# TensorE's side jobs dealt anew over the eight slots of an attention and FP4 feed-forward kernel

## The reference

```python
xn = _layernorm(x)
q  = rope((xn @ Wqa @ Wqb).reshape(b, s, 16, 8))
kv = (xn @ Wkva @ Wkvb).reshape(b, s, 4, 8, 2); k, v = rope(kv[..., 0]), kv[..., 1]
w  = softmax(causal(einsum('bqhd,bkhd->bhqk', q, repeat(k, 4)) * 8 ** -0.5))
attn = einsum('bhqk,bkhd->bqhd', w, repeat(v, 4)).reshape(b, s, 128) @ Wout + bout
h   = silu(fp4_linear(xn, w_gate)) * fp4_linear(xn, w_up)      # 352 hidden features
out = x + attn + fp4_linear(h, w_down)
```

## Time and profile before

| | |
|---|---|
| median of 3 runs | 909.72 us (909.21 to 912.68) |
| profiled execution | 912.46 us, of which the span is 910.7 us |
| mean granted TensorE clock | 0.979 |
| PE busy | 760.9 us, 84% |
| DVE busy | 633.5 us, 70% |
| POOL busy | 595.6 us, 65% |
| ACT busy | 554.4 us, 61% |

### The profile page before, as it was taken

How to read it: one execution, slowest core, us unless ns; L and a number is a source line. 1 busy time by engine, 2 the same in 40 slices (tenths; PEclk the granted TensorE clock), 3 DMA queues, 4 the chain that set the end, 5 groups by cost and what they waited for, 6 DMA issues and landing times.

```text
span 910.7 us, 21907 instructions
## 1 busy us (share of the span) xinstructions
PE 760.9 (84%) x6641; PEld 479.6 (53%) x6733; DVE 633.5 (70%) x1380; ACT 554.4 (61%) x1169; POOL 595.6 (65%) x706
## 2 busy tenths in 40 slices
PE   2366879989897989989897988989898898999785
PEld 1233545656564555646555565645655565656344
DVE  3679877687776867767786778768776877777300
ACT  1122766675756766665675667566666667575761
POOL 3425778776775667857676687666676887664731
PEclk9998999999999999989999999999999999999997
DMA  4312122323223132321222232221223232220000
GB/s 113 92 53 83 46 79 62 89 64 84 56 62 77 29 89 63 89 52 60 72 65 66 54 89 58 75 70 53 60 53 90 63 89 53 70 70 13 15 24 12
DMA packets 66257, 58.28 MB, mean 64 GB/s; under 512 B 17298, under 2 KB 56178, under 8 KB 66170
## 3 DMA queue, kind: packets, MB, share of 16 engines
q1 hardware_dynamic: 66170, 57.04, 23.8%
HBM read 31.81 MB, written 18.61 MB: 55 GB/s over the span
## 4 chain that ended last, share of the span: by engine, by line
PE 40%; ACT 18%; issue 13%; DVE 11%; POOL 9%; another core or an unknown queue 4%; SPq 2%; DMA 1%; DVEq 1%; ACTq 0%; POOLq 0%
PE pv_ps L1036 8%; ACT P L840 6%; PE exp_ps L1017 6%; DVE neg_max L646 5%; PE misc_ps L1103 5%; PE max_ps L1002 5%; POOL P L495 5%; PE misc_ps L1054 4%; PE misc_ps L1064 3%; ACT h_mag L948 2%; PE max_ps L1003 2%; PE misc_ps L1072 2%; PE misc_ps L1101 2%; ACT hqT L886 1%
## 5 line engine op out<-in xcount | busy, mean ns | idle before, releaser
L646 DVE TENSOR_REDUCE neg_max<-max_ps 128x1 f32<-128x512 f32 (+3 forms) x768 | 430.6, 596 | 183.8 <-PE max_ps L1003 182.4
L840 ACT ACTIVATE P<-exp_ps 128x512 f32<-128x512 f32 x512 | 291.7, 599 | 200.2 <-PE exp_ps L1017 103.6
L1017 PE MATMUL exp_ps<-Q,K 128*128 128x128 bf16 (+3 forms) x932 | 211.6, 295 | 25.4 <-ACT P L840 18.3
L1002 PE MATMUL max_ps<-K,Q 128*128 128x384 bf16 (+2 forms) x768 | 200.3, 280 | 35.3 <-DVE neg_max L646 15.6
L1003 PE MATMUL max_ps<-Kd,Q 128*128 128x128 bf16 x1024 | 191.4, 222 | 0.7 <-DVE neg_max L646 0.5
L1036 PE MATMUL pv_ps<-P,V 128*32 128x512 f32 (+3 forms) x2048 | 167.0, 442 | 18.6 <-POOL P L495 12.9
L495 POOL TENSOR_SCALAR_AFFINE_SELECT P<-P 128x512 f32<-128x512 f32 x256 | 153.9, 638 | 19.0 <-ACT P L843 19.0
L1002 PEld LDWEIGHTS max_ps<-K,Q 128*128 128x128 bf16 x768 | 76.9, 100 | 111.8 <-issue 52.2
L1003 PEld LDWEIGHTS max_ps<-Kd,Q 128*128 128x128 bf16 x1024 | 101.0, 99 | 37.2 <-issue 19.3
L1017 PEld LDWEIGHTS exp_ps<-Q,K 128*128 128x128 bf16 x1024 | 79.3, 98 | 73.7 <-ACT P L840 48.4
L1036 PEld LDWEIGHTS pv_ps<-P,V 128*32 128x32 f32 x2048 | 59.5, 110 | 78.9 <-issue 45.5
(11 more groups left out here) (113 smaller groups left out, 1013.5 us busy)
## 6 DMA issues: line engine op xcount, KB each, us to landing
Q<-q_scr SPq DMA_DIRECT2D x64, 224.0 KB
q_scr<-q_split SPq DMA_DIRECT2D x16, 384.0 KB, 2.6
Kd<-K SPq DMA_DIRECT2D x64, 96.0 KB
x_in<-x SPq DMA_DIRECT2D x16, 256.0 KB, 2.9
q_scr<-q_split SPq DMA_DIRECT2D x16, 256.0 KB, 2.9
x_res<-x SPq DMA_DIRECT2D x16, 256.0 KB, 5.4
out<-y SPq DMA_DIRECT2D x16, 256.0 KB, 4.5
K<-k_scr SPq DMA_DIRECT2D x64, 48.0 KB
```

The costliest lines, as they stand in the source:

```text
L646: nc.vector.tensor_reduce(neg_max[:, pr // 4, i, heads[0]:heads[0] + len(heads), pr % 4], max_ps[r % 3][:, 0:len(heads) * n].rearrange("p ...
L840: nc.scalar.activation(P[g % 2][:, hh + r % 2, col:col + 512], ps[:, :], ACT.Exp, scale=SCALE).then_inc(exp_done, 1)
L1002: nc.tensor.matmul(ps[:, col:col + d], Qt, Kt[:, half, g, 0:d], start=True, stop=True)
L1017: last = nc.tensor.matmul(exp_ps[n % 2][:, col:col + width], K[par][:, half, pr // 2, kb * 128:(kb + 1) * 128], Q[par][:, pr, kb * 128:S], ...
```

## The change

- `MISC`: mrow1 from bank 1 to bank 0. Slot 2 has q at point 0, qrot at point 1 and ot1 at point 2; kv goes to slot 3, point 1; onT to slot 4, point 1. The output job is cut into out0 (slot 5, point 0) and out1 (slot 6, point 0), of two token blocks each. xqT and ot0 go to bank 1, mrow0 to bank 0, and hqT0, hqT1 and hqT2 stand at the three points of slot 7.
- Weighted sums: key blocks 0 and 3 in even slots, 1 and 2 in odd ones.
- ACT's h_mag pieces at (6, 2), (6, 4), (7, 0) and (7, 2). The rest of ACT's `extra` is as it was.
- DVE: its reads stand at new places, y is made in halves, and ot0 is read from bank 1.
- SP: the store is two DMAs, one ahead of and one behind `place_max(T, 1, 0)`; POOL's x_bias waits for out1 of the step before.

```diff
 MISC = [
     [[("gate0", 0, 1), ("up0", 1, 1)], [], []],
-    [[("gate1", 0, 1), ("up1", 1, 1)], [("xnT", 1, 2)], [("mrow1", 1, 0)]],
-    [[("q", 0, 2), ("qrot", 1, 2)], [("ot1", 0, -1), ("kv", 1, 2)], []],
-    [[("gate2", 0, 1), ("up2", 1, 1)], [("onT", 1, -1)], []],
-    [[("gate3", 0, 1), ("up3", 1, 1)], [], []],
-    [[("out", 0, -1)], [("xqT", 0, 2)], []],
-    [[("hqT0", 1, 0)], [("ot0", 0, 0), ("hqT1", 1, 0)], [("mrow0", 1, 1)]],
-    [[("hqT2", 1, 0)], [], []],
+    [[("gate1", 0, 1), ("up1", 1, 1)], [("xnT", 1, 2)], [("mrow1", 0, 0)]],
+    [[("q", 0, 2)], [("qrot", 1, 2)], [("ot1", 0, -1)]],
+    [[("gate2", 0, 1), ("up2", 1, 1)], [("kv", 1, 2)], []],
+    [[("gate3", 0, 1), ("up3", 1, 1)], [("onT", 1, -1)], []],
+    [[("out0", 0, -1)], [("xqT", 1, 2)], []],
+    [[("out1", 0, -1)], [("ot0", 1, 0)], [("mrow0", 0, 1)]],
+    [[("hqT0", 1, 0)], [("hqT1", 0, 0)], [("hqT2", 1, 0)]],
 ]
-H_POWERS = [(6, 2), (6, 3), (6, 4), (7, 0)]
+H_POWERS = [(6, 2), (6, 4), (7, 0), (7, 2)]
+PV_BLOCKS = ((0, 3), (1, 2))
...
                 if T.has(-1):
-                    T.misc_wait(sp, misc_read, "out")
-                    sp.dma_start(out[T.batch(-1)].rearrange("(c p) e -> p c e", p=128), y[:, :, :]).then_inc(stored, 16)
+                    store(T, 0)
                 if T.has(1):
                     place_max(T, 1, 0)
+                if T.has(-1):
+                    store(T, 1)
...
-                reduces(2, 2)
+                reduces(2, 2, 3)
                 if T.has(2):
                     T.misc_wait(dve, misc_filled, "qrot")
...
-                reduces(2, 3)
+                reduces(2, 4, 5)
+
+                reduces(3, 0)
                 normalize(T, -1, 1)
-                reduces(2, 4)
+                reduces(3, 1)
+                hidden_max(T, 1)
+                reduces(3, 2)
+                gated(T, 2)
+                reduces(3, 3, 4)
                 if T.has(2):
...
                     nc.vector.tensor_copy(v_stage[:, :, :], ps[:, 256:384].rearrange("p (c n) -> p c n", c=NT)).then_inc(misc_read[1], 1)
-                reduces(2, 5)
-
-                reduces(3, 0, 1)
-                hidden_max(T, 1)
-                reduces(3, 2)
-                gated(T, 2)
-                reduces(3, 3, 4)
+                reduces(3, 5)
+
+                reduces(4, 0, 1)
...
-                    T.wait(dve, stored, 16, -1, 0)
-                    nc.vector.tensor_tensor(y[:, :, :], misc_ps[0][:, :].rearrange("p (c e) -> p c e", c=NT),
-                                            x_bias[:, :, :], ALU.add).then_inc(misc_read[0], 1)
+                    T.wait(dve, stored, 32, -1, 0)
+                    output(T, 0)
                 reduces(5, 3)
...
-                reduces(6, 0, 1, 2, 3)
+                reduces(6, 0, 1, 2)
+                if T.has(-1):
+                    output(T, 1)
+                reduces(6, 3, 4)
                 normalize(T, 0, 0)
-                reduces(6, 4, 5)
-
-                reduces(7, 0, 1, 2)
+                reduces(6, 5)
+
+                reduces(7, 0, 1, 2, 3)
                 if T.has(1):
                     T.wait(dve, h_powers, NT, 1, NT)
                     magnitudes(lambda s, n: T.wait(dve, s, 2, 1, n), h_mag[:, :], h_mags)
-                reduces(7, 3, 4, 5)
+                reduces(7, 4, 5)
...
-                for kb in ((2, 3) if second else (0, 1)):
+                for kb in PV_BLOCKS[second]:
...
-                elif job == "out":
+                elif job in ("out0", "out1"):
                     T.misc_wait(pe, misc_read, "onT")
-                    for c in range(NT):
-                        nc.tensor.matmul(ps[:, tok[c]], onT[:, tok[c]], wout_sb[:, :], start=True, stop=False)
+                    for n in range(2):
+                        c = 2 * int(job[-1]) + n
+                        nc.tensor.matmul(ps[:, tok[n]], onT[:, tok[c]], wout_sb[:, :], start=True, stop=False)
```

More of the change, by code:

```diff
@@ L414, in copy_k, with store @@
                     sp.dma_start(Kd[r:r + MROW, half, gs, :], K[i][r:r + MROW, half, gs, :]).then_inc(qk_loaded[hf], 16)
+            def store(T, n):
+                T.misc_wait(sp, misc_read, f"out{n}")
+                rows = out[T.batch(-1)].rearrange("(c p) e -> p c e", p=128)
+                sp.dma_start(rows[:, 2 * n:2 * n + 2, :], y[:, 2 * n:2 * n + 2, :]).then_inc(stored, 16)
             def place_max(T, off, hf):
@@ L551, in iteration @@
                     T.wait(pool, x_res_loaded, 16, -1, 16)
-                    T.prev().misc_wait(pool, misc_read, "out")
+                    T.prev().misc_wait(pool, misc_read, "out1")
                     nc.gpsimd.tensor_tensor(x_bias[:, :, :], x_res[:, :, :],
@@ L682, in normalize, with output @@
                 nc.vector.tensor_tensor(o_norm[:, :, g, :, :],
-                                        misc_ps[0][:, :].rearrange("p (c n d) -> p c n d", c=NT, d=16)[:, :, :, 0:D],
+                                        misc_ps[1 - g][:, :].rearrange("p (c n d) -> p c n d", c=NT, d=16)[:, :, :, 0:D],
                                         o_inv[:, :, :].rearrange("p (c j) s -> p c (j s)", c=NT).unsqueeze(3).to_broadcast([128, NT, 8, D]),
-                                        ALU.mult).then_inc(misc_read[0], 1)
+                                        ALU.mult).then_inc(misc_read[1 - g], 1)
+            def output(T, n):
+                T.misc_wait(dve, misc_filled, f"out{n}")
+                c = slice(2 * n, 2 * n + 2)
+                nc.vector.tensor_tensor(y[:, c, :], misc_ps[0][:, 0:2 * E].rearrange("p (c e) -> p c e", c=2),
+                                        x_bias[:, c, :], ALU.add).then_inc(misc_read[0], 1)
             def iteration(T):
@@ L757, in iteration @@
                     magnitudes(lambda s, n: T.wait(dve, s, 2, 2, n), x_mag[:, :], x_mags)
-                reduces(3, 5)
-                reduces(4, 0, 1, 2)
+                reduces(4, 2)
                 gated(T, 3)
-                reduces(4, 3)
+                reduces(4, 3, 4)
                 hidden_max(T, 2)
-                reduces(4, 4, 5)
+                reduces(4, 5)
                 reduces(5, 0, 1)
@@ L1037, in weighted_sums @@
                                                 P[g % 2][:, j, P_COL[kb]:P_COL[kb] + width],
-                                                start=(kb == 0 and g % 2 == 0), stop=(kb == NT - 1 and g % 2 == 1))
+                                                start=(kb == 0 and g % 2 == 0), stop=(kb == PV_BLOCKS[1][1] and g % 2 == 1))
                 if second:
@@ L1050, in misc_job @@
                     f = int(job[-1])
-                    if bank == 1:
-                        T.prev().misc_wait(pe, misc_read, "xqT")
+                    T.prev().misc_wait(pe, misc_read, "xqT")
                     last = nc.tensor.matmul(ps[:, 0:F], xqT[T.par(1)][:, tok[f]], wguT[:, int(job[0] == "u"), :], start=True, stop=True)
@@ L1059, in misc_job @@
                 elif job in ("q", "qrot"):
-                    if bank == 0:
-                        T.misc_wait(pe, misc_read, "xnT")
+                    T.misc_wait(pe, misc_read, "xnT")
                     c0 = E * int(job == "qrot")
@@ L1096, in misc_job @@
                         last = nc.tensor.transpose(ps[:, tok[c]], o_norm[:, c, :, :, :].rearrange("p g n d -> p (g n d)"), ident[:, :])
-                elif job == "out":
+                elif job in ("out0", "out1"):
                     T.misc_wait(pe, misc_read, "onT")
-                    for c in range(NT):
-                        nc.tensor.matmul(ps[:, tok[c]], onT[:, tok[c]], wout_sb[:, :], start=True, stop=False)
+                    for n in range(2):
+                        c = 2 * int(job[-1]) + n
+                        nc.tensor.matmul(ps[:, tok[n]], onT[:, tok[c]], wout_sb[:, :], start=True, stop=False)
                         for k, (_, cn) in enumerate(FC):
-                            last = nc.tensor.matmul(ps[:, tok[c]], hqT[0:cn, k, tok[c]], wdT[0:cn, k, :], start=False, stop=(k == 2))
+                            last = nc.tensor.matmul(ps[:, tok[n]], hqT[0:cn, k, tok[c]], wdT[0:cn, k, :], start=False, stop=(k == 2))
                 last.then_inc(misc_filled[bank], 1)
```

5 lines of the change are left out of this document (2 added, 3 removed).

## The result

The changed kernel takes 968.12 us (median of 5 runs, 962.91 to 969.92) beside 910.7 of the kernel before (5 runs): a ratio of 1.0595, 95% interval 1.0565 to 1.0625. The profiled execution is the fastest of the five, 962.91 us, with a span of 961.2 against 910.7 before. The mean granted clock of TensorE fell from 0.979 to 0.940.

A forecast was written before the change was run, and what follows sets the result against it. An iteration was taken as the sum over its eight slots of whichever engine is last in each. Slot changes gave +2.85 us an iteration, +40 over 14 iterations, -2 for two more: +38, 948 us; range 912 to 983.

The forecast's parts named there:

- The mechanism, slot 3: Late kv delays k_rope and ScalarE's cast; PE stands idle before the fifth exp tile; slot 9.9 against 4.93, +5.0 us.
- the waits in slot 5: Slot 5: DVE waits 1.6 us at h_scale for POOL's product of the old h; xqT no longer waits for y.
- the signs named: ScalarE idle some 4 us, k_rope waiting over 5, PE gap over 2, slot 3 near 10, slots 2, 4, 5 under 6.
- The sum at full clock: Slot changes of one iteration, +0.1 +0.6 -2.1 +5.0 -0.4 -2.3 +1.2 +0.75, add to +2.85 us.
- rival B: Clock falls in every slot 3: 14 x 1.2 = 17 us more, 965 us, up to 983; chance 0.25.
- between those rows but nearer the first: Slot 3's new gap, about 2.7 us, set between a 2.87 gap with low clock and a 1.76 gap with full clock.
- PE waits for POOL in slot 4 anyway: Argument against the fallen clock's cost: slot 4 has PE waiting for POOL in any case; no size given.
- A: Stall in slot 3 with the clock kept: 948 us, bounds 912 to 967; chance 0.55.
- Rival C: k_rope ready before ACT needs it, so no slot 3 stall: -1.65 us an iteration, 885 us; chance 0.14.
- Levelled sums at nothing: Pairing key blocks 0+3 and 1+2: even slots lose 0.4 us, odd ones gain 0.4, so no net gain.
- The sum over two slots stays: Weighted sums of an even and an odd slot together take unchanged time, about 1.2 us each after the change.

The follow-up runs named there:

- the run with the cast later: Changed kernel with ScalarE's cast of k_rope behind its fifth exp tile and GpSimd's k_rope and k_rest behind other work: 906.56 us, ratio 0.9904.
- the version with the mask first: The run with the cast later, plus normalize(ot1) earlier, h scales behind slot 5's reductions, GpSimd's causal mask before its h_inv product, h_mag pieces later: 869.66 us, ratio 0.9515.

## Why the prediction was right, and where it was wrong

**The mechanism, slot 3: right.** ScalarE's stall (3.86 us, "some 4" foreseen), k_rope's wait (7.17), PE's gap before the fifth exp tile (2.72, foreseen 2.7) and the slot (10.11 at full clock, foreseen 9.9) are as worked out; so are the waits in slot 5, and TensorE no longer waits for y there. Of the signs named, one failed by a little: slot 2 is 6.1 to 6.2 us, not under 6. Moving kv alone into the kernel before gives ratio 1.0506, and back out of the changed one 1.0004.

**The sum at full clock: right.** The slots of T=13, foreseen and measured: 6.1 and 6.03; 7.2 and 6.61 (this iteration had 6.07 before, so it is +0.5 of the +0.6 foreseen); 5.85 and 6.21; 9.9 and 10.11; 5.7 and 5.76; 5.7 and 5.74; 7.75 and 7.42; 5.1 and 5.23. The step grew by 2.61 us, foreseen 2.85; single slots miss by up to 0.6 us, and these misses nearly cancel.

**The clock: rival B happened, not the 948 us with the clock kept.** The failing step is the weighing of the new gap as "between those rows but nearer the first", from which I still gave the kept clock 0.55 against 0.25. Behind 12 of 14 gaps of 2.54 to 2.72 us it fell. All four turns of the loop in the kernel before spoke for that, and I showed only one of them; "PE waits for POOL in slot 4 anyway" had no row behind it. But length was not the whole of the rule either: four gaps of 2.44 to 2.87 us of the changed kernel kept the clock. The measured 968 lies above the upper bound of A, 967, and is in the range by B alone. B's price, 1.2 us an iteration and 965 us in all, was near it, in part by luck: slots 3 and 4 lost 2.2 together in T=11 (11.68 + 6.39 against 10.11 + 5.76), less in others, 20 in all. The low clock lasts into slot 4, where 0.81 is its mean; I had priced it in the sums alone, 17 us. Against that stands what I had not foreseen: at the loop's turns the changed kernel kept the clock that the kernel before lost, so slots 0 and 1 behind them take 11.5 us together in place of 12.2 to 13.3, 4 us in all. The Trainium skill, page "TensorE: Matmul & The Clock Gate", section "HAM oscillation — how this bites in real kernels", has a loop in which each pass starts cold, and the waits of that loop are longer than this gap. The low clock in each pass is what came here, but for two passes of fourteen.

**Rival C, 885 us without the stall: wrong in its price.** With TensorE's stall taken out in two ways, the runs give 906.56 and 916.54. C foresaw -1.65 us an iteration; T=13 of the run with the cast later has -0.13 (50.37 against 50.50). Two terms failed. The larger is slot 3, put at +1.5 and measured at +2.45 (4.94 to 7.39): gate2's wait for normalize, which I had named in the walk through the slot and left out of C's sum. Without it slot 3 is 6.36, +1.4. The second is slot 6, put at +0.5 and measured at +1.0: I took off the wait at h_scale together with the stall, as if kv's lateness caused it. The wait itself was as foreseen (GpSimd's product ends 5.74 into slot 5, foreseen 6.0; VectorE arrives at 4.4; 1.38 us), but it comes from slot 5 being shorter than GpSimd's queue, and behind it stands a second holder that I had not named, the chain of h, h_inv and causal mask on GpSimd, 2.6 + 1.2 + 2.6 + 2.4 us.

**Levelled sums at nothing: wrong.** "The sum over two slots stays" is true of PE's time and not of the slots': worth 1.2% in the kernel before. My reference iteration hid it, too: I took one with slot 2 at 7.95, as in four of T=1 to 12, while the other eight have 8.2 to 8.7.

What stays open: why gaps of the same length drop the clock in one place or iteration and not in another, and whether kv in slot 2 would be better still in the version with the mask first. No run tried either.

## What to carry to other kernels

Before moving a producer, look up on every engine the place of its first consumer, and what stands in order behind that consumer: a cast of 0.3 us at the wrong place cost 2.7 us of TensorE and then its clock. When a wait is removed and the slot doesn't shrink, there is a second holder; follow the engine's whole queue up to the instruction that the slot's last work needs, and reorder that queue. A new deal of jobs has to be judged with queues whose order fits it: this one stands at ratios from 1.06 to 0.95 by four placements (the cast with k_rope, normalize, the scales, the mask with h_mag).

## What the runs showed of the hardware

- Gaps of TensorE of 2.72 us in slot 3 of the changed kernel were followed by the 1.2 GHz level in ten of ten cases, gaps of 2.54 us in two of four, and gaps of 2.44 to 2.87 us at the loop's turn in none of four. With useless products in the slot 3 gap the kernel was 21 us faster.
- These two tensor_scalars of VectorE (h_scale and x_scale, SBUF to SBUF in fp32) do not run beside a GpSimd tensor_tensor that started first. 88 columns took 1.63 us in place of 0.20. I found the same afterwards where nobody had looked for it, and with one buffer: x_scale, 32 columns, has a median of 0.17 us in the kernel before and 1.04 in the changed one, where GpSimd's x_bias (1.27 us) now runs beside it. In the kernel before only two of its sixteen records are long, 1.03 and 1.17 us, and they are the two that began after an x_bias and before its end. The two records of T=12 in the changed kernel end 0.04 us apart:

```profile
764.08 1.27 POOL L560 TENSOR_TENSOR x_bias<-x_res,bout_sb 128x512 f32<-128x512 f32 x1
764.15 1.24 DVE L628 TENSOR_SCALAR x_scale<-x_max 128x32 f32<-128x32 f32 x1
```

Such a wait stands in none of the lists of waits here. It shows as one shape's duration that is longer than the same shape's elsewhere, and by its end lying at another engine's end.
